# Opening of a two-layer transformer kernel: ScalarE's convolution evictions spread between projections, and unit-matrix turns put before and behind TensorE's first turn

## What is computed

```python
x = x + L0_ffn(L0_cond(x, cond_2048[:, None, :], b), ...)   # causal depthwise convolution + b; then attention and experts
x = x + L1_ffn(L1_cond(x, cond_2048, ada_w, ada_b, ...), ...)  # adaLN attention and FFN; then low-rank experts
# inside L0_cond
y = conv_general_dilated(x, w, padding=[(K - 1, 0)], feature_group_count=D) + b
# inside L0_ffn
h = rmsnorm(hidden, attn_norm_w)
q, k, v = h @ q_w.T, h @ k_w.T, h @ v_w.T          # 16 query heads, 4 key/value heads of 128
q, k = rope(rmsnorm(q)), rope(rmsnorm(k))
hidden = hidden + softmax(causal(q k^T / sqrt(128))) v @ o_w.T
# inside L1_cond
ada = (timestep_embed @ ada_w + ada_b)              # six vectors of 256 for each sequence
```

## Time and profile before

| | us |
|---|---|
| three runs | 675.26, 677.07, 678.24 |
| median | 677.07 |
| the profiled execution's own time | 674.97 |
| its span, first to last instruction | 673.2 |
| TensorE busy | 618.3 (92%) |
| VectorE busy | 392.7 (58%) |
| ScalarE busy | 329.3 (49%) |
| GpSimd busy | 188.4 (28%) |
| mean granted TensorE clock | 0.977 of full |

### The profile page before, as it was taken

The page is one execution under the profiler, slowest core; times in us unless marked ns, Lnnn a source line. Parts: engine busy times, 40 slices in busy tenths (PEclk is TensorE's granted clock), DMA queues, the critical chain, the costliest instruction groups (busy, mean ns, idle before and its releaser), DMA issues.

```text
span 673.2 us, 13706 instructions
## 1 busy us (share of the span) xinstructions
PE 618.3 (92%) x5634; PEld 518.6 (77%) x5634; DVE 392.7 (58%) x735; ACT 329.3 (49%) x836; POOL 188.4 (28%) x194
## 2 busy tenths in 40 slices
PE   3688999999998899999899999999999999889997
PEld 1566877787877788888777888788888887668776
DVE  3678778777887647765483362352423517852553
ACT  2586667756674135433236554454454343365440
POOL 0564433243423123542043240121102003542000
PEclk9589999999999989999999999999999999999999
DMA  8440000000000344445100221101000002101023
GB/s 271 172 188 2 1 2 1 3 1 2 1 2 2 134 139 129 141 140 172 64 1 1 63 66 30 32 18 48 1 1 1 2 1 63 32 1 32 1 64 125
DMA packets 12606, 36.28 MB, mean 54 GB/s; under 512 B 2152, under 2 KB 3688, under 8 KB 11936
## 3 DMA queue, kind: packets, MB, share of 16 engines
q1 hardware_dynamic: 12304, 34.36, 15.8%
q10 hardware_dynamic: 240, 1.05, 0.6%
HBM read 34.29 MB, written 1.11 MB: 53 GB/s over the span
## 4 chain that ended last, share of the span: by engine, by line
PE 75%; DVE 9%; ACT 8%; issue 3%; DMA 3%; POOL 2%; SPq 0%; DVEq 0%; ACTq 0%
PE ps L1298 18%; PE ps L1299 17%; PE ps L1300 16%; PE ps L1418 9%; PE ps L1583 4%; ACT raw_s L663 2%; PE ps L1741 2%; PE ps L1375 2%; DMA xT<-in_x_T 2%; ACT hid L621 1%; PE ps L1403 1%; PE ps L1571 1%; PE ps L1389 1%; ACT work L656 1%; PE ps L1327 1%
## 5 line engine op out<-in xcount | busy, mean ns | idle before, releaser
L1165 DVE SCALAR_TENSOR_TENSOR strm_lo<-ps,col,strm_hi 128x512 fp32r<-128x512 f32 x32 | 24.0, 750 | 113.3 <-ACT strm_hi L779 112.1
L475 POOL TENSOR_TENSOR w_lo<-raw_w,w_hi 128x1024 fp32r<-128x1024 f32 x20 | 49.4, 2486 | 133.5 <-ACT w_hi L589 110.7
L1298 PE MATMUL ps<-w_hi,act_hi 128*128 128x512 f32 x160 | 65.8, 411 | 5.9 <-ACT junk L582 3.2
L763 ACT ACTIVATE work<-ps,col 128x512 f32<-128x512 f32 x64 | 44.2, 690 | 49.1 <-PE ps L1300 48.9
L1418 PE MATMUL ps<-raw_w,raw_s 128*128 128x256 f32 x256 | 61.1, 383 | 4.5 <-ACT raw_s L663 4.5
L1298 PE MATMUL ps<-act_hi,w_hi 128*128 128x512 f32 x160 | 63.0, 394 | 2.2 <-POOL act_lo L537 1.6
L1299 PE MATMUL ps<-w_lo,act_hi 128*128 128x512 f32 x160 | 63.9, 399 | 0.0
L1300 PE MATMUL ps<-w_hi,act_lo 128*128 128x512 f32 x160 | 63.8, 399 | 0.0
L1300 PE MATMUL ps<-act_hi,w_lo 128*128 128x512 f32 x160 | 62.3, 390 | 0.0
L1299 PE MATMUL ps<-act_lo,w_hi 128*128 128x512 f32 x160 | 62.3, 389 | 0.0
L1418 PEld LDWEIGHTS ps<-raw_w,raw_s 128*128 128x128 f32 x256 | 46.3, 190 | 12.8 <-ACT raw_s L663 7.7
(11 more groups left out here) (187 smaller groups left out, 1467.5 us busy)
## 6 DMA issues: line engine op xcount, KB each, us to landing
raw_w<-in_w_attn SPq DMA_DIRECT2D x16, 512.0 KB, 4.6
raw_s<-in_w_moe SPq DMA_DIRECT2D x11, 384.0 KB, 4.4
work<-comb_dram SPq DMA_DIRECT2D x10, 256.0 KB, 3.9
work<-comb_dram SPq DMA_DIRECT2D x18, 128.0 KB, 2.9
raw_w<-in_w_qkv SPq DMA_DIRECT2D x4, 512.0 KB, 12.7
raw_w<-in_w_o SPq DMA_DIRECT2D x1, 2048.0 KB, 7.6
raw_s<-in_w_ffn SPq DMA_DIRECT2D x8, 256.0 KB, 2.7
bd<-in_w_ada SPq DMA_DIRECT2D x1, 1536.0 KB, 6.3
```

Of the source, the lines that this page charges most:

```text
L475: G.tensor_tensor(flat(w_lo[:, slot]), raw, flat(f32(w_hi[:, slot])), ALU.subtract).then_inc(s_piece_lo, 1)
L763: A(dst[:, h * BANK:(h + 1) * BANK], src, ACT.Identity, bias=c_(b, 4 * j + h)).then_inc(s_q1_copied, 1)
L1165: V.scalar_tensor_tensor(flat(strm_lo[:, n % SS]), ps[:, 4 + n % 2, :], c_("bv", 4 * (u // CHUNKS) + h), flat(f32(strm_hi[:, n % SS])), AL ...
L1298: mm(dst, ah, bh, start=start and i == 0, stop=False, **flags)
```

## The change

On ScalarE the eight evictions of `Y_REST` no longer stand in a row before the first take of a projection. One stands there, one behind each of the projections 0 to 4, and two behind the sixth. On TensorE 32 turns of the unit matrix go to bank 1 before `turn_y(0)`, and 12 behind it. The waits are as before. VectorE, GpSimd and SyncE have the same instructions in the same order.

```diff
-            def take_conv(tiles):
-                for q in range(PAIR):
-                    for b in range(BT):
+            def take_conv(tiles, parts):
+                for q, b in parts:
                         A(*conv_out(q, b, tiles), ACT.Copy).then_inc(s_y_act, 1)
+
+            QB = [(q, b) for q in range(PAIR) for b in range(BT)]
...
-            take_conv(Y_FIRST)
+            take_conv(Y_FIRST, QB)
             take_y(0)
             for i in range(3, NPROJ):
                 piece0_hi(i)
-            take_conv(Y_REST)
+            take_conv(Y_REST, QB[0:1])
             for s in range(TILES + 1):
                 if s < TILES:
                     take_proj(s, 0)
+                if s == 0:
+                    take_conv(Y_REST, QB[1:2])
...
                 if s < TILES:
                     for k in range(1, 3):
                         take_proj(s, k)
+                        if s == 0:
+                            take_conv(Y_REST, QB[k + 1:k + 2])
...
                 if s < TILES:
                     for k in range(3, NPROJ):
                         take_proj(s, k)
+                        if s == 0:
+                            take_conv(Y_REST, QB[k + 1:k + 2] if k < NPROJ - 1 else QB[k + 1:])
                     take_qkT(s)
...
+            keep_warm(32, 1)
             turn_y(0)
+            keep_warm(12, 1)
             for s in range(TILES + 1):
```

## The result

| | before | after |
|---|---|---|
| runs, us | 675.26, 677.07, 677.41, 678.24 | 685.93, 687.09, 687.43, 687.87 |
| median, us | 677.24 | 687.26 |
| profiled execution's own time | 674.97 | 687.43 |
| its span | 673.2 | 685.5 |
| second tile's projections begin | 56.80 | 65.89 |

The ratio is 1.0155, with a 95% interval from 1.0124 to 1.0186. The changed kernel is slower by 10.0 us, from median to median; the two profiled executions lie 12.5 us apart, since the one of the kernel before was 2.3 us faster than its median. I had forecast +8.7, 685.8 us in a range of 680.0 to 689.0. The new lines are L1346 for the unit-matrix turns, L1354 for the turn of a tile, L1305 to L1307 for the projections, L1459 for the adaLN product, L1382 for the turns of queries and keys, L1396 for the scores.

What follows compares the result with a forecast made beforehand. TensorE holds 75% of the chain, so the start of the second tile's projections decides. The product starts at 49.2, ends at 59.4; projections begin at 65.5 instead of 56.80: 677.07 + 8.7 = 685.8 us, range 680.0 to 689.0.

Steps and rivals of the forecast that it cites:

- The last eviction sets the product's start: The adaLN product waits for all sixteen ScalarE evictions, so it starts at 47.55 + 1.6 = 49.2 us instead of 45.46.
- The clock is low by then, and the product cannot bring it back: After at least 7.6 us idle, TensorE runs the whole adaLN product at 1.2 GHz, taking 10.2 us.
- the convolution's row: The convolution, 32 columns like the product, filled 2.88 of 3.00 us at clock 0.50 without bringing the clock back.
- ScalarE's stretch from the first eviction to the last take stays 15.2 us: No ScalarE instruction is added and nothing waits, so first eviction to the values' take stays 47.56 - 32.33 = 15.2 us.
- The 32 turns shift the opening by 1.6 us: Before tile 0's turn, 32 turns take 5.3 to 5.8 us in a 3.60 us gap, shifting ScalarE's whole stretch 1.6 us.
- Rival 3: Turns do not raise TensorE's clock: shift 3.3, second tile's projections at 69.2, +14.4, 691.5 us; chance 0.09.
- Rival 4: Not slower: VectorE's rope decides, beginning at 40.1; second tile's projections start at 55.4, -1.4, 675.6 us; chance 0.05.
- From T to the second tile's projections: From the product's end T = 59.4, 22 turns, ScalarE's last copy and the scores take until T + 6.1 us.
- six projections "at most 2.2 us": Six TensorE projections after the last weight piece need at most 2.2 us, from twelve that took 4.4.
- Nothing behind 56.8 gives it back: After 56.8 us the opening's +8.7 us is not recovered, as TensorE has no idle time worth it there.

Runs made afterwards that it cites:

- e4_early: The changed kernel with ScalarE's last seven evictions earlier, two behind each of the first three projections and one behind the fourth: 684.10 us, ratio 1.0114 to the kernel before.
- e1_spread_only: The changed kernel without the 44 turns, so the spread evictions alone: 683.61 us, ratio 1.0104 to the kernel before.
- e7: The changed kernel with 16 turns instead of 32 before the turn of tile 0: 683.08 us, ratio 1.0099 to the kernel before.
- e3_bridge: The changed kernel with 72 more unit-matrix turns in TensorE's idle time before the adaLN product: 680.08 us, ratio 1.0055 to the kernel before.
- e9: e8 with the adaLN product made wide, its 32 columns taken four times over (128): 672.87 us, ratio 0.9946 to the kernel before.
- e10: The kernel before with the wide (128-column) adaLN product and GpSimd's clearing of bd behind tile 1's norms: 674.02 us, ratio 0.9966.
- e11: The changed kernel with the wide (128-column) adaLN product: 683.32 us, ratio 1.0097 to the kernel before.
- e8: Against the kernel before: evictions spread four, two, two; 26 turns and two rope results' turns before the adaLN product; clearing behind tile 1's norms: 677.24 us, ratio 1.0024.
- e5: The kernel before with GpSimd's clearing of bd behind the norms of tile 1 instead of tile 0: 677.64 us, ratio 1.0014.
- e2: The kernel before with the 44 turns around the turn of tile 0 and no spread evictions: 679.65 us, ratio 1.0054.
- e6: The kernel before with 44 unit-matrix turns between the bias products and the convolution: 679.07 us, ratio 1.0052.

## Why the prediction was right, point by point

- **The last eviction sets the product's start**: forecast 49.2, seen 49.06. Shown by e4_early, where the product followed the eviction to 44.64 ahead of two takes, and by e1_spread_only.
- **The clock is low by then, and the product cannot bring it back**: forecast 10.2 us, seen 10.42, again in e1, e4 and e7. That the clock is the reason is shown by e3_bridge (5.92 us at the same place). That the product's form matters is shown by e9, e10 and e11 beside e8, e5 and the changed kernel. But the reason that I gave, the convolution's row, does not carry the step, and that part was luck. In four other profiled executions the same convolution brought the clock back by itself (see e4_early). It is also another case: its weights are 64x64 and its rows followed each other 0.02 us apart at the low clock, the product's 0.22. No row of the kernel before that I went by settled whether this product would bring the clock back; only the runs do.
- **ScalarE's stretch from the first eviction to the last take stays 15.2 us**: seen, now to the last eviction, 48.96 - 33.33 = 15.6 us. A take lasted 1.6 to 1.7 us, not 1.48, when an eviction stood before it. A small miss, covered by the stretch starting only 1.0 us later than before (33.33 against 32.33) and not 1.6: that 49.2 and 49.06 agree so well is two errors that cancel.
- **The 32 turns shift the opening by 1.6 us**: seen 1.3. Counted from the convolution's end, the turn of tile 0 was over after 29.53 - 23.95 = 5.6 us instead of 28.54 - 24.29 = 4.3. This term hangs on the clock at which the execution happens to stand there: in e2 and e4 the turns found it full and took 3.71 us.
- **Rival 3, turns do not raise the clock**: fell. The clock rose at about 27.5 with nothing but turns on TensorE since 23.88, and in e1_spread_only at 61.6 with nothing but turns since 57.47. Here the rule that the Trainium skill gives (TensorE: Matmul & The Clock Gate, Part 4: PE-mode transpose), that the full clock does not engage for transposes, does not agree with the trace: they brought the clock from 0.50 to 1.00. How soon they do is another matter: behind the product of the changed kernel 4.9 us of turns had not done it.
- **Rival 4, rope decides**: rope began at 39.51 (forecast 40.1) and ended 8.7 us before it was of use.
- **From T to the second tile's projections**: forecast 6.1 us, seen 65.89 - 59.29 = 6.6. I had the 22 turns speed up after 3.6 to 4.6 us and end after 4.4; they were slow throughout and ended after 64.23 - 59.29 = 4.9.
- **A bound that was too low**: six projections "at most 2.2 us". The twelve that it was taken from ran at both clocks. At the low one they start 0.43 us apart (at 41.74 and 42.17, for instance), which is 2.6 us for six. It decides nothing: at the full clock the last six ended at 40.45, and TensorE was idle for 8.61 us.
- **The step that was wrong**: "Nothing behind 56.8 gives it back" was meant to say that the rest stays as it is, and it did not. The 44 instructions cost 2.5 us in the tile loop, a term that my sum lacks. Another 0.9 us went behind the tile loop, where the clock was low from 607.7 to 611.1: VectorE's rows stand 11.50 us later than before ahead of that stretch and 12.36 behind it. That is one execution's clock.
- **Why the total came out near all the same**: luck. Against the profiled execution my sum gives 683.7, and the changed kernel's took 687.43: 0.4 us too little in the opening, 2.5 in the tile loop, 0.9 behind it. But I added the full 8.7 us to the median of the kernel before, which is some 2 us above its profiled execution. That execution kept the full clock through the product; many others of the same kernel are slower with a lower mean clock, probably because they lose it there and so pay already a part of what the changed kernel always pays (argued, see e5_clear_later). Counting that part twice made up for some 2 of the 3.7 us that the sum lacked.

## What to carry to other kernels

When work is moved off the front of an engine's queue, look for the semaphore that counts all of it: the spread started rope 2 us earlier and cost 7.5 us, because a product waited for the whole set and then met a low clock. A TensorE product of few columns between whole weight loads should be read at both clock levels; where it must stand behind or before idle time, repeating its 32 columns to 128 cost next to nothing here and kept the clock. Adding instructions to TensorE can move a stall in a loop far behind, so compare a loop's period before and after, and vary the count. And a sum worked out against one execution holds for the median only if that execution is typical where the change acts.

## What the runs showed of the hardware that I had not expected

- A product of 32 columns between loads of 128x128 weights not only failed to raise the clock; it lost it while TensorE was busy without a gap: 2 us into it in e8_rework, about 3 us in e2_turns_only, 3.6 in e5 and e6, 5 in e3_bridge. Of the six profiled executions in which it had the full clock from its start or within 0.5 us of it, only that of the kernel before kept it. The same product with 128 columns held it in e9 and e10, and raised it after 5.9 us in e11. It is not the 32 columns alone: the convolution, 32 columns with weights of 64x64, raised the clock in four executions and held it in e6_turns_first.
- Two additions of 64 columns on VectorE lasted 2.64 us beside GpSimd's clearing and 0.42 without it. The Trainium skill (SBUF — State Buffer, SBUF: two separate sides) has an exclusive lock of a port pair that the two engines share: of a GpSimd instruction and a VectorE instruction of a kind that needs the pair, the one that starts first has it for its whole length, and the other is blocked. The trace agrees: in the kernel before, the first addition ended 0.07 us after the clearing (55.89 and 55.82), and in e5_clear_later, without the clearing beside it, the wait was gone. The bias before it, another kind of instruction, ran beside the clearing and took its usual 0.57 us.
- 44 further TensorE instructions cost 2.0 to 2.7 us in tiles 1 to 6 wherever they stood in the opening; 26, 28 and 116 cost nothing. In the five kernels that lost time, two packets of the instruction queue q8 stood 3.5 to 3.8 us apart in the tile with the longer gap, in the others 7.4 to 7.8.
